# Delta attention: wide key-norm products and four steps issued at other places

## What is computed

```python
kn = k_t / max(norm(k_t), 1e-12)
r = clip(v_t - S @ kn, -1, 1)
S = a_t * S;   S = S + b_t * outer(kn, v_t - kn @ S);   o = S @ q_t
R = aR_t * R;  R = R + g_t * outer(kn, r - kn @ R);     o = o + R @ q_t
```

## Time and profile before

| what | value |
|---|---|
| median of three runs | 3460.13 us |
| the profiled execution's own time | 3470.97 us |
| its span in the profile | 3469.2 us |
| TensorE busy (matmuls) | 3172.4 us, 91% |
| VectorE busy | 2475.7 us, 71% |
| ScalarE busy | 1446.3 us, 42% |
| POOL busy | 898.0 us, 26% |
| mean granted clock of TensorE | 0.963 |
| chain that ended last | TensorE 36%, VectorE 32%, issue 6% |

### The profile page before, as it was taken

One profiled execution on the slowest core, in us unless ns is written; L12 is line 12 of the kernel. 1 busy time (PEld: TensorE's weight loads), 2 busy tenths in 40 slices (PEclk: granted clock), 3 DMA queues, 4 the chain that ended last, 5 costly groups with the idle time before them and its releaser, 6 DMA issues.

```text
span 3469.2 us, 145126 instructions
## 1 busy us (share of the span) xinstructions
PE 3172.4 (91%) x64386; PEld 2372.4 (68%) x64386; DVE 2475.7 (71%) x5588; ACT 1446.3 (42%) x3274; POOL 898.0 (26%) x1045
## 2 busy tenths in 40 slices
PE   6885999998699999999999999999999999978999
PEld 4664999987466666666666766667666666656666
DVE  6983111120688888888888888888888888876997
ACT  1322222221354554455455544454445544533443
POOL 2444222212132223222322232322332233221000
PEclk9996999999899999999999999999999999999999
DMA  2217666666000000000000000000000000010100
GB/s 68 57 67 238 187 186 187 191 205 175 25 10 9 10 8 11 8 10 8 11 8 10 8 11 8 10 8 8 11 9 10 8 12 9 8 49 10 33 28 16
DMA packets 97900, 168.32 MB, mean 49 GB/s; under 512 B 15240, under 2 KB 71688, under 8 KB 97024
## 3 DMA queue, kind: packets, MB, share of 16 engines
q1 hardware_dynamic: 76688, 136.01, 12.0%
q0 software_dynamic: 19440, 21.97, 4.5%
q10 hardware_dynamic: 1152, 1.06, 0.1%
HBM read 118.80 MB, written 38.09 MB: 45 GB/s over the span
## 4 chain that ended last, share of the span: by engine, by line
PE 36%; DVE 32%; issue 6%; ACT 1%; POOL 0%; DVEq 0%; ACTq 0%; POOLq 0%
DVE da_eGn L1291 8%; DVE da_z L1290 8%; PE da_unit L1752 5%; PE da_C L1922 5%; PE da_unit L1952 4%; PE da_unit L1838 3%; PE da_A L1893 3%; PE da_B L1909 2%; PE da_A L1870 2%; PE da_B L1900 2%; DVE da_M L1314 2%; PE da_B L1882 2%; PE da_unit L1818 2%; PE da_B L1883 1%; DVE da_eGn L1294 1%
## 5 line engine op out<-in xcount | busy, mean ns | idle before, releaser
L1134 POOL TENSOR_TENSOR da_M<-da_M,da_decay 128x512 f32<-128x512 f32 x256 | 261.3, 1046 | 798.2 <-DVE da_TT L1296 439.8
L1548 ACT COPY da_Ub<-da_U 32x256 f32<-32x256 f32 x992 | 399.3, 403 | 16.6
L1291 DVE TENSOR_TENSOR da_eGn<-da_eGn,da_z 128x30 f32<-128x30 f32 (+14 forms) x960 | 328.4, 342 | 33.0
L1290 DVE TENSOR_TENSOR da_z<-da_eGn 128x30 f32<-128x30 f32 (+14 forms) x960 | 329.7, 343 | 27.6
L1752 PE MATMUL da_unit<-early_buffer,da_xnT 128*128 128x512 f32 x512 | 285.5, 644 | 10.4 <-DVE da_sp L1232 6.4
L1922 PE MATMUL da_C<-da_Ub,da_Km 128*64 128x256 f32 x1984 | 288.7, 410 | 0.8 <-issue 0.4
L1539 ACT COPY da_U<-da_A 128x256 f32<-128x256 f32 x256 | 95.3, 372 | 425.9 <-PE da_A L1893 425.8
L842 PEld LDWEIGHTS le_ps_qkv<-le_scr,le_up 128*128 128x128 f32 x2272 | 265.5, 193 | 4.8 <-ACT le_scr L672 1.8
L842 PE MATMUL le_ps_qkv<-le_scr,le_up 128*128 128x128 f32 x2272 | 267.5, 276 | 1.2 <-ACT le_scr L672 1.2
L1893 PEld LDWEIGHTS da_A<-da_W,da_TT 32*32 32x32 f32 x8192 | 127.9, 106 | 188.3 <-DVE da_W L1309 67.4
L1760 PE MATMUL da_unit<-da_xnT,early_buffer 128*128 128x128 f32 x2048 | 242.2, 277 | 9.9 <-ACT da_eGn L1531 9.9
(11 more groups left out here) (315 smaller groups left out, 6979.4 us busy)
## 6 DMA issues: line engine op xcount, KB each, us to landing
le_up<-in_upT SPq DMA_DIRECT2D x71, 1024.0 KB, 5.0
le_scr<-moe_slots SPq DMA_DIRECT2D x71, 129.0 KB, 4.2
le_down<-in_downT SPq DMA_DIRECT2D x8, 1024.0 KB, 12.7
early_buffer<-in_x SPq DMA_DIRECT2D x16, 256.0 KB, 4.0
moe_acc<-le_y SPq DMA_DIRECT2D x32, 128.0 KB, 2.5
da_x<-moe_acc SPq DMA_DIRECT2D x128, 32.0 KB, 1.8
stream<-da_xz SPq DMA_DIRECT2D x128, 32.0 KB, 1.6
stream<-da_y POOLq DMA_DIRECT2D x128, 32.0 KB, 2.9
```

The source lines that it names most:

```text
L1134: ins = nc.gpsimd.tensor_tensor(st_, st_, decay[:, par, rec, 2 * g:2 * g + 2].rearrange("p a b -> p (a b)").unsqueeze(2).to_broadcast([P, ...
L1290: c.link(tt(t, Xm[:, s + 1:C, s:s + 1].to_broadcast([P, below, s]), Xm[:, s:s + 1, 0:s].to_broadcast([P, below, s]), ALU.mult))
L1291: c.link(tt(Xm[:, s + 1:C, 0:s], Xm[:, s + 1:C, 0:s], t, ALU.add))
L1548: ins = nc.scalar.copy(Ub[rows_of(b), :, :, b, :], U[rows_of(b), rec])
```

## The change

Six edits, all in the delta attention:

1. TensorE's `norms_of_keys` issues one product per head pair, 128 tokens wide: eight instead of 32.
2. VectorE's `state_rows` of group 0 moves from the head of period i + 1 to the tail of period i, ahead of `update(i, 3, 1)`.
3. VectorE's `gates` is split: the bias addition (`gates_in`) follows `norms_of_keys`, the rest (`gates_out`) follows `update(i, 0, 0)` and precedes `norm_last`.
4. Steps 1 and 2 of the substitution move ahead of `clipped(i, par, 2)`.
5. TensorE's `gram(n, pn, 1)` moves ahead of `state_predicted(i, par, 2)`.
6. On POOL the residual addition leaves `norms` for a function `residual`, called behind `factors`.

```diff
--- before.py
+++ after.py
@@ -1114,11 +1114,13 @@
             def norms(n):
                 need(pool, var_ready, n * 2 + 1)
                 nc.gpsimd.tensor_tensor(rstd[:, 0:1], ve[:, 0:1], mhalf[:], ALU.pow).then_inc(rstd_ready, 1)
+                need(pool, var_ready, n * 2 + 2)
+                nc.gpsimd.tensor_tensor(rstd[:, 1:2], ve[:, 1:2], mhalf[:], ALU.pow).then_inc(rstd_ready, 1)
+
+            def residual(n):
                 need(pool, z_ready, n + 1)
                 need(pool, xz_stored, n * (16 * B))
                 nc.gpsimd.tensor_tensor(xz[:], x[:], z[:], ALU.add).then_inc(xz_ready, 1)
-                need(pool, var_ready, n * 2 + 2)
-                nc.gpsimd.tensor_tensor(rstd[:, 1:2], ve[:, 1:2], mhalf[:], ALU.pow).then_inc(rstd_ready, 1)
 
             def scaled_values(i, par, g):
                 need(pool, v_ready, i * 2 + (g // 2 + 1))
@@ -1170,6 +1172,8 @@
                     scaled_values(i, par, 3)
                 if prepare:
                     factors(i + 1, 1 - par)
+                if norm:
+                    residual(i + 2)
                 if state:
                     rescale(i, par, 3)
                 if prepare:
@@ -1191,6 +1195,7 @@
             pc.link(nc.gpsimd.memset(neg[:], -1.0))
             pool.wait_ge(cleared, 1)
             norms(0)
+            residual(0)
             every_period(period)
             put_out(LAST)
             for t in range(1, TRIPS):
@@ -1231,9 +1236,11 @@
                 cols = slice((u % 2) * 512, (u % 2 + 1) * 512)
                 tt(sp[:, u // 2, cols], un[:, RATE_BANK[u]], ba[:, u // 2, cols], ALU.add).then_inc(a_ready, 1)
 
-            def gates(n):
+            def gates_in(n):
                 need(dve, bg_psum, n + 1)
                 tt(bg[:], un[:, 0, 0:2 * H], bbg[:], ALU.add).then_inc(bg_ready, 1)
+
+            def gates_out(n):
                 need(dve, bge_ready, n + 1)
                 c.link(nc.vector.tensor_scalar(nsig[:], nsig[:], 1.0, -1.0, ALU.add, ALU.mult))
                 nc.vector.reciprocal(nsig[:], nsig[:]).then_inc(sig_ready, 1)
@@ -1376,8 +1383,6 @@
                 state, prepare, norm, put = flags(i)
                 n, pn = i + 1, 1 - par
                 carry = state and i < LAST
-                if state:
-                    state_rows(i, 0)
                 if norm:
                     norm_first(i + 2)
                 if prepare:
@@ -1386,14 +1391,16 @@
                     norm_second(i + 2)
                 if prepare:
                     norms_of_keys(n)
+                    gates_in(n)
                 if state:
                     clipped(i, par, 0)
                 if carry:
                     update(i, 0, 0)
+                if prepare:
+                    gates_out(n)
                 if norm:
                     norm_last(i + 2)
                 if prepare:
-                    gates(n)
                     products(n, pn, 1, 1)
                 if state:
                     state_rows(i, 1)
@@ -1428,12 +1435,13 @@
                     gram_out(n, pn, 0)
                     gram_out(n, pn, 1)
                     triangle_in(n, pn)
+                    substitute(1, 3)
                 if state:
                     clipped(i, par, 2)
                 if carry:
                     update(i, 2, 0)
                 if prepare:
-                    substitute(1, 6)
+                    substitute(3, 6)
                 if norm:
                     add_bias(i + 2, 2)
                 if prepare:
@@ -1457,6 +1465,7 @@
                 if prepare:
                     substitute(12, C - 1)
                     triangle_out(n)
+                    state_rows(n, 0)
                 if carry:
                     update(i, 3, 1)
 
@@ -1791,8 +1800,7 @@
                     need(pe, q_ready, n * 2 + 1)
                     need(pe, k_ready, n * 2 + 2)
                 for hp in range(half * HB, (half + 1) * HB):
-                    for b in range(B):
-                        ins = mm(un[rows_of(b), 1, 2 * hp:2 * hp + 2], sq[:, hp, rows_of(b)], sel[:], start=True, stop=True)
+                    ins = mm(un[:, 1, 2 * hp:2 * hp + 2], sq[:, hp, :], sel[:], start=True, stop=True)
                 if half == 1:
                     ins.then_inc(n_psum, 1)
 
@@ -2077,10 +2085,10 @@
                     gram(n, pn, 0)
                 if put:
                     result(i - 1, 1)
+                if prepare:
+                    gram(n, pn, 1)
                 if state:
                     state_predicted(i, par, 2)
-                if prepare:
-                    gram(n, pn, 1)
                 if put:
                     result(i - 1, 2)
                 if state:
```

## The result

The changed kernel takes **3494.1 us** (median of four runs, 3493.71 to 3496.88) against 3461.27 for the kernel before: **1.0087 times**, with a 95% interval of 1.0075 to 1.0099. It is slower. Forecast were 3448 us and a range of 3418 to 3478; the result lies above both. The profiled execution has a span of 3491.9 us and its own time is 3493.71.

What follows compares the result with a forecast made beforehand. TensorE, busy 65.8 of 69.8 us a period, was taken as the bound, VectorE nearly full. Terms of -11.1 (full-clock periods), +0.2 (falling-clock periods) and -1 gave -12 us on 3460.13: 3448 us, range 3418 to 3478.

Steps and rivals of the forecast that it cites:

- kind A: Periods between transposes with granted clock 1.00 throughout, 13 of 31; forecast -0.71 us up to turn_x and -0.14 after.
- kind B: Periods whose clock falls to 0.50 soon after the transpose, 18 of 31; forecast +0.15 us up to turn_x, -0.14 after.
- inside the wait, so the norms cost nothing here: Full-clock periods: TensorE reaches the next solve 0.51 us later, within its 1.00 us wait for the clipped W.
- rival 1: Wide two-column products make the clock fall in every period: 3474 us, 3484 with issue waits kept; decides from six more falls; chance 0.17.
- -0.14 a period: Middle of each period: substitution steps fill VectorE's 1.02 us wait before clipped 2; 0.19 us kept, less short-wait periods.
- 18 x (1.3 - 0.58): Key norms in the 18 falling-clock periods: wide products cost 1.3 us each period, vanished issue waits give back 0.58.
- 18 x -0.58, 13 x -0.71 and -1: Up to turn_x: earlier W gains 0.58 us in falling-clock periods; full-clock ones gain 0.71; first and last periods give -1.
- rival 2: The clock stops falling because issue waits and half the idle go: 3413 us, half of it 3430; chance 0.15.
- Less the periods whose wait was short: Deduction from the 0.19 us kept by the moved substitution steps: there clipped 2 comes up to 0.16 us later.
- other end: Alternative for TensorE's issue waits between L1893 and L1900, 0.58 us a falling-clock period: they stay instead of going.
- The number of B periods moves by more than four: Listed sign that the forecast is wrong: the count of periods with a falling clock, 18 of 31, changes beyond four.
- Rival 4: Key norms: the eight wide products are as cheap as their number says, term 0 or below: 3425 us; chance 0.07.

## Why the prediction was wrong

**The step that failed** is the key norms' effect on the clock, which the sum put at nothing: it kept 13 periods of kind A and 18 of kind B and made the wide products a matter of busy time alone. Price and place of the products were right, and so was "inside the wait, so the norms cost nothing here": 0.9 us a half were forecast and 0.96 measured, and in the five periods whose clock held turn_x moved from 13.23 to 12.35 us (-0.88, forecast -0.71), which is also where it lies with narrow products (12.35, edits 2 and 3). But there are five of these now, not 13, and more of the falls are long ones. By count the change lost more than the six periods from which rival 1 "decides". The two kernels that differ in the moved columns alone, 1.0087 and 0.9973, put 39 us on it.

A second term failed with it: "-0.14 a period" for the middle, edits 4 and 5, which cost instead. By edits, with the forecast's own terms beside the runs:

| edits | terms of the sum | runs |
|---|---|---|
| 1 | 18 x (1.3 - 0.58), +13 us | +39 us within the change, +47 alone |
| 2 and 3 | 18 x -0.58, 13 x -0.71 and -1, -21 us | -27 us (-11 and -10 alone) |
| 4 to 6 | 31 x -0.14, -4 us | +18 us on top of 2 and 3, +27 with the clock held |
| all | -12 us | +30 us |

**Rival 1, the clock falls in every period**, is what happened, in 26 of 31. It had a chance of 0.17 and prices of 3474 and 3484 us. I held against it that "the idle shrinks" and that issue waits go. Both did, and the clock fell all the same. Idle time does count (edit 2 alone, 18 falls to 6), but it was not the whole measure: what the products move counts as well. Its price was also low by 10 to 20 us; it still counted a gain for edits 4 and 5, each of which costs. The six periods that fell without an issue wait, which I used against rival 2, should have counted for this one.

**Kind B.** Where the mean clock is below 0.97, turn_x went from 14.55 to 14.75 us: +0.20, forecast +0.15. In the periods with a shorter fall (0.97 and 0.98) it went from 13.93 to 13.13. So up to turn_x the term holds for the long falls and was too dear for the short ones. Over the whole period it does not hold: periods with a long fall take 71.61 us for 70.22, with a short one 70.14 for 69.73, where the sum had them unchanged. Edits 4 and 5 have their price there as well. (The falls of the kernel before begin 3.0 to 7.7 us after the transpose, not 5 to 8.)

**Edits 2 and 3** came out near their terms alone (11 and 10 us) and at 27 together. The idle ahead of the solve went from 1.10 to 0.50 and the wait for U went, as written. What the sum left out is that fewer periods fall with them: 18 become 10. So the term of edit 2 was right partly by luck: it was to gain in 18 periods of kind B, and with edit 2 alone there are six. Rival 2, "the clock stops falling", came true only where the key norms moved 64 columns, with 2 falls of 31, and 3427 us where it had 3413 for the whole change.

**Edit 4** was forecast at -0.14 a period (with what edit 5 brings) and costs 13 us. The failed step is reading the wait before clipped 2 from one period (1.02 us) where the mean is 0.48. "Less the periods whose wait was short" was the right worry, but clipped 2 comes 0.56 us later on average and not "up to 0.16"; and behind a late clipped 2 stands TensorE's second solve of group 2, which the prediction did not name.

**Edit 5** was to let VectorE's last masking start 0.27 us earlier, and the sum has no term of its own for it: "TensorE's total is the same". Its busy time is; its waits are not, and it costs 13 us alone. That issue waits would stay, only elsewhere, is the "other end" that I had written for the head of the period. From 955 to 3060 us they are 43.4 us before and 43.3 after, but these are two effects that cancel by chance: edit 1 takes the ones at the key norms away for good (27.8 us with edit 1 alone, 35.0 in the kernel with edits 2 and 3 and 64 columns), and edit 5 adds about as many after 33 us of a period (0.57 to 1.13 us).

**The signs that I had listed**: two runs of eight records of about 0.9 us, the wait of 0.5, and no wait for U, all came. VectorE's wait moved to clipped 3 (0.80 us on average in the change) only in part: 0.63 stays before clipped 2. Periods at clock 1.00 are 0.47 shorter (69.07 for 69.54) and not 0.85; the head gives 1.05 and the second half takes 0.58 back. "The number of B periods moves by more than four" came true, 18 to 26, and was the mark of a wrong forecast. No issue wait reappeared in the head of a period.

**Edit 6** was forecast to do nothing, and does nothing.

**Fewer is not cheaper.** Rival 4 is refuted: four wide products take 0.96 us a half where 16 narrow ones took 0.36. This is also where the rule of the Trainium skill, TensorE: Matmul & The Clock Gate, section LDWEIGHTS, parts in two: for the wide loads this case's trace agrees with a price by loaded columns (some 120 ns a record with 2 moved columns, 129 with 64), for the narrow ones, 11 ns a record, it does not. The same page, section Packing small matmuls, says that small tiles run at the same time in one array; the trace of the narrow ones agrees with that.

## What to carry to other kernels

Where TensorE's clock falls in some periods of a loop and not in others, look at what its instructions move through the array in the stretch ahead of the falls and not only at how long they keep it busy: here products that load 128 columns to move two count as busy in the profile, and the clock fell in 26 of 31 periods, in two with 64 moved columns. Widening what they move cost 0.05 us a half and gave back 39 us in all. So count the falls before and after as a term of the sum, not as a constant. And read the wait that an edit is meant to fill in all periods: its mean, and how often it is zero, before its longest.

## What the runs showed of the hardware

**A busy TensorE whose clock falls.** In the changed kernel TensorE is busy throughout the stretch ahead of a fall, save one idle of 0.5 us, and its clock falls in 26 of 31 periods; with the same idle and 64 moved columns for two it falls in 2 of 31. The Trainium skill, TensorE: Matmul & The Clock Gate, section Why this matters for your kernels, puts a fall down to idle gaps between bursts of products. The trace does not agree that this is all: with edit 1 alone and 64 columns the gap is the longer one (1.11 us) and the falls are fewer (9 of 31). That the gap has a part is shown too: halved by edit 2 alone, 18 falls become 6. Why the moved columns matter to the clock no run shows.

**Moved columns cost little.** Eight records of 128 stationary columns take 0.96 to 0.98 us with 2 moved columns and 1.03 with 64. Narrow ones, 32 records, take 0.36 with 2 columns and 0.59 with 64 (1636.88 to 1637.47 in the kernel with edits 2 and 3), and still that kernel gained: 0.9892 for 0.9923 (intervals 0.9874 to 0.9909 and 0.9906 to 0.9941), with 2 falls for 10.

```profile
1636.88 0.67 PE L1798 MATMUL da_unit<-da_sel,da_eG 128*32 128x64 f32 x32
1637.47 0.65 PE L1903 MATMUL da_B<-da_U,da_gm 32*32 32x64 f32 x32
```

**Issue waits have no recorded cause.** What makes them was not found. They come in the stretches of many small products, and they can go as well as come: 43.4 us in the kernel before, 27.8 with eight wide products for 32 narrow ones (edit 1 alone), 58.3 with only one gram moved (edit 5 alone).
